# Diagonal tiles of B written by DMA through a DRAM image, in the two scan layers

## The reference

```python
seq = x.reshape(B, C, L).transpose(0, 2, 1)            # L = 1024 places, DIM = 192
proj = seq @ W_proj.T + b_proj
x_in, delta = proj[..., :DIM], proj[..., DIM:2 * DIM]
Bm, Cm = proj[..., 2*DIM:2*DIM + 16], proj[..., 2*DIM + 16:]   # D_STATE = 16
delta = jax.nn.softplus(delta + dt_bias)
def step(h, inp):
    d_t, x_t, b_t, c_t = inp
    h = exp(d_t[..., None] * A) * h + (d_t * x_t)[..., None] * b_t[:, None, :]
    y_t = einsum('bdn,bn->bd', h, c_t)
y = scan(step) + x_in * D
out = y @ W_out.T + b_out
```

## Time and profile before

| | us |
|---|---|
| median of 3 runs | 4305.36 |
| profiled execution, span of the core | 4308.6 |
| DVE busy | 3432.3 |
| POOL busy | 2659.4 |
| PE busy | 3710.7 |
| ACT busy | 2105.8 |

### The profile page before, as it was taken

How to read it: one execution, slowest core, us unless ns; L and a number is a source line. 1 busy time by engine, 2 the same in 40 slices (tenths; PEclk the granted TensorE clock), 3 DMA queues, 4 the chain that set the end, 5 groups by cost and what they waited for, 6 DMA issues and landing times.

```text
span 4308.6 us, 119610 instructions
## 1 busy us (share of the span) xinstructions
PE 3710.7 (86%) x49136; PEld 2266.0 (53%) x49136; DVE 3432.3 (80%) x3492; ACT 2105.8 (49%) x2803; POOL 2659.4 (62%) x973
## 2 busy tenths in 40 slices
PE   4994899899999996789889888899898888888897
PEld 4994666666666664344444444444444444444443
DVE  6564567667576663699998998999999989999997
ACT  2331343444444443556555555555565555555563
POOL 1111121111211210599899999999999999999998
PEclk9997899999999998799999999999999999999999
DMA  9624142242332330553543543544535535435433
GB/s 101 85 44 108 54 124 81 85 119 70 95 109 69 105 91 25 120 116 79 125 106 83 125 102 92 125 94 103 122 84 120 112 79 124 109 79 130 103 87 83
DMA packets 296948, 416.40 MB, mean 97 GB/s; under 512 B 31369, under 2 KB 185741, under 8 KB 296385
## 3 DMA queue, kind: packets, MB, share of 16 engines
q1 hardware_dynamic: 295440, 408.35, 41.7%
q10 hardware_dynamic: 978, 0.34, 0.0%
HBM read 267.09 MB, written 91.16 MB: 83 GB/s over the span
## 4 chain that ended last, share of the span: by engine, by line
PE 27%; DVE 16%; issue 12%; ACT 3%; POOL 1%; DVEq 1%; DMA 0%; ACTq 0%; POOLq 0%
DVE ssm_h L1136 11%; PE ssm_u_ps L818 10%; PE ssm_y_ps L831 10%; PE ssm_scratch L848 4%; DVE ssm_b_diag L1160 3%; PE ssm_scratch L858 1%; DVE ssm_stats L1143 1%; POOL ssm_h L1216 1%; ACT ssm_decay L967 1%; PE ssm_u_ps L893 1%; DVE ssm_y_sb L1165 1%; ACT ssm_xn L994 1%; PE ssm_scratch L873 1%; PE ssm_scratch L867 0%; DVEq L1128 0%
## 5 line engine op out<-in xcount | busy, mean ns | idle before, releaser
L1216 POOL TENSOR_TENSOR ssm_h<-ssm_h,ssm_c_rep 128x2048 f32<-128x2048 f32 x384 | 1745.4, 4550 | 107.3 <-DVE ssm_h L1136 99.6
L967 ACT ACTIVATE ssm_decay<-ssm_delta_rep,ssm_a_neg 128x1024 f32<-128x1024 f32 x768 | 863.7, 1145 | 592.1 <-DVE ssm_h L1136 589.3
L818 PE MATMUL ssm_u_ps<-ssm_b_diag,ssm_dx_t 64*64 64x128 f32 x24576 | 865.7, 282 | 262.3 <-DVE ssm_h L1136 182.6
L818 PEld LDWEIGHTS ssm_u_ps<-ssm_b_diag,ssm_dx_t 64*64 64x64 f32 x24576 | 696.3, 137 | 698.9 <-issue 694.6
L1136 DVE TENSOR_TENSOR_SCAN ssm_h<-ssm_decay,ssm_h,ssm_u_ps 128x512 f32<-128x512 f32 x768 | 944.3, 1257 | 132.5 <-PE ssm_u_ps L818 131.4
L1136 DVE TENSOR_TENSOR_SCAN ssm_h<-ssm_decay,ssm_u_ps 128x512 f32<-128x512 f32 x768 | 887.2, 1195 | 35.8 <-ACT ssm_decay L967 16.9
L831 PE MATMUL ssm_y_ps<-ssm_h,ssm_state_sum 128*64 128x512 f32 x3072 | 798.1, 643 | 8.0 <-POOL ssm_h L1216 8.0
L1752 ACT ACTIVATE l_probs<-l_work 128x532 f32<-128x532 f32 (+1 forms) x384 | 217.6, 567 | 560.7 <-PE l_work L1606 554.0
L1160 DVE TENSOR_TENSOR ssm_b_diag<-ssm_b_t,ssm_lane 128x2048 f32<-128x2048 f32 x128 | 454.0, 3549 | 22.7 <-ACT ssm_b_t L1022 22.7
L2004 POOL TENSOR_TENSOR l_rstd<-l_var_eps,l_minus_half 96x2 f32<-96x2 f32 x16 | 11.1, 695 | 586.6 <-DVE l_var_eps L1841 586.6
L831 PEld LDWEIGHTS ssm_y_ps<-ssm_h,ssm_state_sum 128*64 128x64 f32 x3072 | 196.8, 144 | 326.3 <-issue 311.9
(11 more groups left out here) (163 smaller groups left out, 5554.7 us busy)
## 6 DMA issues: line engine op xcount, KB each, us to landing
ssm_c_rep<-ssm_c_by_state SPq DMA_DIRECT2D x256, 512.0 KB, 6.5
ssm_delta_rep<-ssm_delta SPq DMA_DIRECT2D x384, 128.0 KB, 5.9
l_qk_parts<-l_qk SPq DMA_DIRECT2D x48, 768.0 KB, 4.8
ssm_x<-x_after_l SPq DMA_DIRECT2D x32, 768.0 KB, 5.8
ssm_x_res<-x_after_l SPq DMA_DIRECT2D x192, 128.0 KB, 4.3
l_x<-x SPq DMA_DIRECT2D x64, 192.0 KB, 9.1
x_after_l<-l_x SPq DMA_DIRECT2D x64, 192.0 KB, 4.1
l_x<-x_after_l SPq DMA_DIRECT2D x16, 768.0 KB, 5.5
```

Source lines behind the costliest of these rows:

```text
L818: made = nc.tensor.matmul(u_ps[64 * par:64 * par + 64, ring("u", w), r, at:at + 128], dx_t[rows, db, 2 * win + k, 64 * g:64 * g + 64], b_d ...
L967: nc.scalar.activation(decay[:, 2 * (s % 2) + npi, :], delta_rep[:, db, :], ACT.Exp, scale=a_neg[:, n.layer, col:col + 1]).then_inc(decay_ ...
L1216: nc.gpsimd.tensor_tensor(view, view, c_rep[:, 2 * q:2 * q + 2, :], ALU.mult).then_inc(c_applied, 1)
```

## The change

The products on DVE go. `b_diag` is laid out anew, [128, 4, 64, 32] instead of [128, 4, 8, 2, 128]: lane j of 64, then 32 values. The moving side of a product now reads 64 pieces of 2 values (8 bytes), 128 bytes apart, where it read 128 values side by side.

B goes by way of a DRAM tensor `b_dram` of [4, 128, 544], cleared once by a DMA at the start. `store_b` writes, for each npq and lane p, the 32 values into the first 32 of row p. A row is 544 values long. `load_diagonal` reads the same memory with rows of 512: row i of a block of 16 lanes then begins 32 i values earlier than the stored row, so that its values appear at column 32 i, with zeros around. That is the diagonal block; 8 blocks of 16 lanes make a group. The zeros of `b_diag` outside the blocks are written once, by a memset.

```diff
+BLOCK = 16
+        b_dram = nc.dram_tensor(f"{tag}_b_blocks", [4, 128, BLOCK * 32 + 32], F32).ap()
+                def store_b(n):
+                    if not n.first:
+                        for npq in range(4):
+                            sp.wait_ge(diag_loaded[npq], n.count(128, 0))
+                            sp.sem_inc(b_store_seen, 1)
+                    sp.wait_ge(b_kept, n.count(1, 1))
+                    sp.dma_start(b_dram[:, :, 0:32].rearrange("q p v -> p q v"), b_t[:, :, :]).then_inc(b_stored, 16)
+
+                def load_diagonal(n, npq):
+                    if not n.first:
+                        sp.wait_ge(u_filled, before(n).count(8 * S_STEPS, 8 * (8 + npq) + 8))
+                        sp.sem_inc(diag_read, 1)
+                    flat_rows = b_dram[npq].rearrange("p v -> (p v)")
+                    for blk in range(128 // BLOCK):
+                        first = blk * BLOCK * (BLOCK * 32 + 32)
+                        j0 = BLOCK * blk % 64
+                        sp.dma_start(b_diag[BLOCK * blk:BLOCK * (blk + 1), npq, j0:j0 + BLOCK, :].rearrange("p j v -> p (j v)"),
+                                     flat_rows[first:first + BLOCK * BLOCK * 32].rearrange("(p v) -> p v", p=BLOCK)
+                                     ).then_inc(diag_loaded[npq], 16)
...
                     if not is_last(n):
                         store_c(m)
                         load_delta(m, 0)
+                        store_b(m)
                         sp.wait_ge(c_stored, m.count(32, 32))
                         sp.sem_inc(c_store_seen, 1)
+                        sp.wait_ge(b_stored, m.count(16, 16))
+                        sp.sem_inc(b_store_seen, 1)
+                        load_diagonal(m, 0)
                         load_c(m, 0)
+                        load_diagonal(m, 1)
                         sp.wait_ge(decay_made, n.count(TILES_S, 16))
                         sp.sem_inc(rep_free, 1)
                         load_delta(m, 1)
+                        load_diagonal(m, 2)
                         load_c(m, 1)
+                        load_diagonal(m, 3)
...
-                        pe.wait_ge(diag_made, n.count(4, npq + 1))
+                        pe.wait_ge(diag_loaded[npq], n.count(128, 128))
...
-                                                            b_diag[rows, npq, 4 * win + 2 * k + g, par, :], start=True, stop=True)
+                                                            of_part(npq, rows, win, k, g, par), start=True, stop=True)
...
-                    nc.scalar.activation(b_t[:, :], scratch[:, 0:256], ACT.Copy).then_inc(drained, 1)
+                    if not n.first:
+                        act.wait_ge(b_stored, n.count(16, 0))
+                    nc.scalar.activation(b_t[:, :, :].rearrange("p q (c i) -> p q c i", i=2),
+                                         scratch[:, 0:256].rearrange("p (c z q i) -> p z q c i", z=2, q=4, i=2)[:, 0],
+                                         ACT.Copy).then_inc(drained, 1)
+                    await_drained(act, f)
+                    act.sem_inc(b_kept, 1)
...
-                    for npq in range(4):
-                        diagonals(n, npq)
+                    nc.vector.memset(b_diag[:, :, :, :], 0.0).then_inc(diag_cleared, 1)
...
-                    if w in (17, 19, 21, 23) and not last:
-                        diagonals(after(n), w // 2 - 8)
```

More of the change, by code:

```diff
@@ L520, in ssm_layers @@
         b_rows = sb("b_rows", [64, HALF])
-        b_t = sb("b_t", [128, 256])
+        b_t = sb("b_t", [128, 4, 32])
         c_rows = sb("c_rows", [128, HALF])
-        b_diag = sb("b_diag", [128, 4, 8, 2, 128])
+        b_diag = sb("b_diag", [128, 4, 64, 32])
         delta_rep = sb("delta_rep", [128, 3, L])
@@ L536, in ssm_layers @@
         ident = sb("ident", [128, 128])
-        lane = sb("lane", [128, 128])
         state_sum = sb("state_sum", [128, 64])
@@ L580, in ssm_layers @@
         dx_made = sem("dx_made")
-        diag_made = sem("diag_made")
+        blocks_cleared = sem("blocks_cleared")
+        b_kept, b_stored, b_store_seen = sem("b_kept"), sem("b_stored"), sem("b_store_seen")
+        diag_read, diag_cleared = sem("diag_read"), sem("diag_cleared")
+        diag_loaded = [sem(f"diag_loaded{npq}") for npq in range(4)]
         rows_seen = sem("rows_seen")
@@ L686, in in_order, with of_part @@
             return t[:, 256 * w:256 * w + 256].rearrange("p (r k j) -> p r k j", k=2, r=2)
+        def of_part(npq, rows, win, k, g, par):
+            first = 16 * win + 8 * k + 4 * g + 2 * par
+            return b_diag[rows, npq, :, first:first + 2]
         def res_rows(t, e):
             return t.rearrange("(q c) h w -> c q (h w)", c=64)[:, :, HALF * e:HALF * e + HALF]
-        N_FIRST, N_REST = 14, 11
+        N_FIRST, N_REST = 13, 11
         def of_slot(n, name):
@@ L759, in prologue @@
                     store_c(n)
+                    sp.wait_ge(blocks_cleared, 16)
+                    store_b(n)
+                    sp.wait_ge(diag_cleared, 1)
+                    sp.wait_ge(b_stored, 16)
+                    load_diagonal(n, 0)
                     sp.wait_ge(c_stored, 32)
                     load_c(n, 0)
+                    load_diagonal(n, 1)
                     load_c(n, 1)
+                    load_diagonal(n, 2)
+                    load_diagonal(n, 3)
                 def early(n):
@@ L1109, in _ @@
                 act.dma_start(ident[:], consts["ident"]).then_inc(first_loaded, 16)
-                act.dma_start(lane[:], consts["lane"]).then_inc(first_loaded, 16)
+                act.dma_start(b_dram.rearrange("q p v -> p q v"), consts["nothing"].to_broadcast([128, 4, BLOCK * 32 + 32])
+                              ).then_inc(blocks_cleared, 16)
                 act.dma_start(w_x[0][0:C], ws[0]["w_x"][0:C]).then_inc(first_loaded, 16)
@@ L1151, in channel_moments @@
                     last.then_inc(moments_made, 1)
[L1153 to L1161, removed]
                 def keep_y(n, db):
@@ L2025, in shape_constants @@
     out["state_sum"] = (p[:, None] % 64 == np.arange(64)[None, :]).astype(np.float32)
-    out["lane"] = np.repeat(p[:, None] % 64 == np.arange(64)[None, :], 2, 1).astype(np.float32)
+    out["nothing"] = np.zeros((1, 4, BLOCK * 32 + 32), np.float32)
     out["ones"] = np.ones((1, 2, 2, 512), np.float32)
```

## The result

The changed kernel took 4328.65 us (median of 13 runs, 4312.33 to 4334.28) against 4308.59 (13 runs, 4302.04 to 4316.21) on the same chips: ratio 1.0042, 95% interval 1.0031 to 1.0052. 4179 was forecast, faster by 3%. The profiled execution took 4313.48 us, span 4311.7. It is one of the quickest of the 13, so the trace accounts for 3 of the 20 us that lie between the medians.

A forecast was written before the change was run, and what follows sets the result against it. Three nearly full engines waiting on each other, with SP's chain in the cycle, were taken as the bound. Gain 3.1 + 1.2 = 4.3 us a pass, times 30, less 3: 126, so 4308.6 to 4182.6, median 4179; range 4085 to 4330.

The forecast's parts named there:

- What goes: DVE's four products leave each pass: 14.2 us less work on DVE and 8 us less on POOL.
- What is late next: The blocks, by SP's chain from its first store: B stored at 18.0, window 2's fill 3.1 us earlier.
- the landing of the second group: Second eight block loads, issued by 27.1, land about 1 us behind C at 30.0; window 2's fill comes 3.1 us earlier.
- the fourth group: Last eight block loads of a pass: issues end 38.9 us after SP's first store; no landing was given.
- Half of the half-clock stretch, 1.2 us: PE's fill and sum at half speed after idleness cost 2.4 us; half of it counted as gained each pass.
- PE's strided reading, no cost: Reading 8-byte pieces 128 bytes apart leaves PE's fills at 1.04 us; rival of a doubled fill: 4725, chance 0.04.
- The first pass, 3 us: B's store, eight issues and their landing replace DVE's 9.06 us of products: 3 us more, bounds -3 and +10.
- The sum: 30 passes at 4.3 us give 129, less 3 for the first pass: 126 us gained, so 4179.
- the gain is eaten: At 0.66 us per block issue and B landing in 3.3, C of step 2 lands at 51.3: 4293, chance 0.10.
- Slower by SP: SP's issues bind: from 0.63 or 0.68 us a block, step 2's apply_c starts later; 4372 at 0.70; chance 0.14.
- The fixed 2.0 us: Fixed part of a DMA; paid in series by eight block loads, 24 us up to window 2's fill (4900); overlap expected.
- The ceiling: If only the engines had a say, a pass comes near 71 us; rival of more gain: 4101, chance 0.14.

The follow-up runs named there:

- 2nd group first: Changed kernel with the second group's eight block loads issued ahead of C's load for step 0: 4343.35 us, ratio 1.0093 to the kernel before.
- residual behind C: Changed kernel with only the residual's six loads and their wait moved behind C's rows of step 3: 4220.78 us, ratio 0.9803 to the kernel before.
- the two experiments: Changed kernel with PE reading contiguously (values wrong): 4301.69 us; kernel before with PE reading strided pairs (values wrong): 4327.82 us.
- residual last: Changed kernel with the residual's six loads and their wait moved behind the last group of block loads: 4241.58 us, ratio 0.9849 to the kernel before.
- both last: Changed kernel with image stores and residual loads behind the last block group, and B's store ahead of delta's loads: 4282.18 us, ratio 0.9946 to the kernel before.
- The blocks go elsewhere: Changed kernel with block loads after the first pass sent to a DRAM tensor, PE reusing the first diagonals unwaited: 4377.45 us, ratio 1.0166 to the kernel before.

## Why the prediction was wrong, point by point

- *What goes*: right. POOL's additions in an ordinary pass take 1.27 to 1.32 us; in the whole span DVE's busy time fell by 409 us and POOL's by 237; over 31 passes that is 7.6 of POOL's time in each, where 8 were said.
- *What is late next*: the right place, the blocks at window 2, and nearly the right times for SP: medians 18.2 for B's landing (18.0 said), 22.2 for the first group's last issue (21.9), 23.6 for C's (23.15), 27.5 for the second group's (27.1). Two errors cancel in them: B's store landed in 1.8 us, not 3.3, but was issued at 15.9, 1.2 us later than said. Of that, 0.8 is the choice of the pass: delta's loads end at 15.4 in the median pass of both kernels, and at 14.65 in the one that was counted from. The rest is 0.5 us of SP between delta's last issue and B's.
- **The step that failed is the landing of the second group: "queued behind a megabyte of C and land about 1 us after it: 30.0".** C landed at 29.8 (29.0 said) and the blocks at 32.2, 2.4 us after it. The fill of window 2 won 0.8 us in the median, not 3.1. "2nd group first" shows that it is C in front that holds them up: without it they landed at 28.0, 1.4 us behind their last issue instead of 4.7.
- **A second step failed, and by the medians it alone would have kept most of the gain away: the fourth group is followed only to the end of its issues (38.9), never to its landing.** It landed at 45.2 (issued to 40.3), where the fill of window 6 had stood at 46.0 and was to go at 46.0 - 4.3 = 41.7. So this gate leaves 0.8 us of the 4.3, however early window 2 is filled. C's third pair, named as a limit near a gain of 5.7 with its landing at 46.0, landed at 49.1; its `apply_c` had stood at 51.3 in the median, which leaves 2.2. "2nd group first" and "residual behind C" in the table show it: window 2 comes at 28, and PE waits at a later group.
- *Half of the half-clock stretch, 1.2 us*: nothing. PE's last fill of the old pass ended near 28 as said, and with the blocks 2.2 us late PE stood still for 4.4 us in the median instead of 2; the clock fell as before.
- *PE's strided reading, no cost*: a fill takes 1.18 to 1.26 us instead of 1.10. 19 to 27 us in all, by the two experiments. The Trainium skill, "SBUF — State Buffer", section "Door 1: The DMA port swizzle", gives full bandwidth at two hits per line, and in the same place has a penalty for each step to a new line, which I left aside; I took the first for PE's reads. The rows show some 10% more for a fill at two hits, so the measurement decides.
- *The first pass, 3 us*: 8.6, the first image store is at 1897.27. Half I had not seen: DVE's `ssm_a_neg`, made from a constant that ACT's queue loads, came at 1735.98 instead of 1731.45. In that queue the DMA that writes zeros over the DRAM image (landed in 9.7 us) is new; that it is the cause was not tried. In the first pass PE then waits 5.40 and 5.64 us for the first two groups.
- *The sum*: 30 passes at 79.18 us in the mean instead of 79.37 give 6, the first pass takes 8.6: +3, as the two spans have it. The other 17 us between the medians lie between executions, and no trace shows their place.
- *The rivals*: "the gain is eaten" was the nearest in size, by another mechanism: not by the issues' price (0.46 us for a block in the median, below the 0.49 taken). "Slower by SP" had the right chain and looked for its limit in C's third pair alone, at 0.63 us an issue; that limit did decide "residual last" and "both last". The fixed 2.0 us that the prediction weighed were not paid in series (the section that it names for them speaks of DMAs issued by GpSimd; these are SP's): eight blocks went out in 3.7 us.
- *The ceiling*: "near 71 us" if only the engines had a say was right (70.2). I took SP's order as given, and so the 126 us as all that was to be had.

## What to carry to other kernels

Work that moves from an engine to DMA joins an in-order queue, and its price is that queue's order: list each consumer's deadline in the pass, all of them, and issue by deadline. A load that waits (here the residual, for its own image's store) belongs behind everything that doesn't. A gain at the first late gate is capped by the next ones; before believing a sum of a few us over a passage of this kind, take the new work out wholly once and look what the engines would allow.

## What the runs showed of the hardware

- A small transfer lands late where large ones are still under way ahead of it in the queue. The second group's last block landed 4.7 us behind the end of its issue with a megabyte of C ahead of it, and 1.4 with C behind it. B's store, 64 KB in pieces of 128 bytes, landed in 1.8 us in the median, 11 us after the 768 KB load of the next image was issued, and in 3.8 where it followed that load by 5 us ("residual last"). The changed kernel's line L757, from issue to landing:
```profile
DMA to landing us min/median/max: 1.8/1.8/3.4
```
- The same 32 KB load costs SP 0.46 us an issue towards SBUF and 0.62 towards DRAM (medians of eight: 3.71 us in the changed kernel, 4.95 in "The blocks go elsewhere").
- PE's clock: behind 4.47 and 4.60 us without work the next fill took 1.99 us, at the lower level of 1.2 GHz (granted clock 0.50 in the 5.5 us from 3183.1 on); behind 2.43 us ("residual behind C") it took 1.19, at the full 2.4 GHz (1.00).
